# Two graph layers on one core: z_hi and z_lo side by side in one aggregation matmul, degree summed by ScalarE

## What is computed

```python
def _L0(x, adj, W):                      # B=8, N=1024, F=256
    deg = jnp.sum(adj, axis=-1, keepdims=True)
    agg = jnp.einsum('bij,bjf->bif', adj, x) / jnp.maximum(deg, 1e-6)
    out = jnp.einsum('bnf,of->bno', jnp.concatenate([x, agg], axis=2), W)
    return relu(out)
def _L1(X, A, kernel, bias):
    Ah = A + eye(N)
    dh = rsqrt(jnp.sum(Ah, axis=-1))
    An = dh[:, :, None] * Ah * dh[:, None, :]
    return relu(jnp.einsum('bnm,bmf,fc->bnc', An, X, kernel) + bias)
x = layernorm(x + _L0(x, adj, L0_gnn_W))
x = layernorm(x + _L1(x, adj, L1_gnn_kernel, L1_gnn_bias))
```

## Time and profile before

| | |
|---|---|
| median of 3 runs | 513.65 us (513.21 to 514.17) |
| profiled execution, its time | 514.48 us |
| its span, first to last instruction | 512.3 us |
| PE busy | 494.2 us, 96%, 3072 matmuls |
| DVE busy | 388.8 us, 76% |
| ACT busy | 244.3 us, 48% |
| DMA | 59.78 MB, 16 engines 32.7% busy |

### The profile page before, as it was taken

The page is one execution under the profiler, slowest core; times in us unless marked ns, Lnnn a source line. Parts: engine busy times, 40 slices in busy tenths (PEclk is TensorE's granted clock), DMA queues, the critical chain, the costliest instruction groups (busy, mean ns, idle before and its releaser), DMA issues.

```text
span 512.3 us, 8698 instructions
## 1 busy us (share of the span) xinstructions
PE 494.2 (96%) x3072; PEld 446.1 (87%) x3072; DVE 388.8 (76%) x1020; ACT 244.3 (48%) x483; POOL 0.7 (0%) x6
## 2 busy tenths in 40 slices
PE   4999999999999999999999999999999999999992
PEld 3899889988899888998889988998889988899872
DVE  4788487984889847987679858798397984898656
ACT  5735436374283542635444553636437364263312
POOL 0000000000000000000000000000000000000000
PEclk9999999999999999999999999999999999999997
DMA  8944401644018240372305531064401614020002
GB/s 280 377 153 166 157 8 41 210 159 164 0 56 278 75 164 0 104 265 67 137 0 174 223 119 58 0 246 164 164 0 41 246 41 164 0 83 1 0 1 82
DMA packets 15978, 59.78 MB, mean 117 GB/s; under 512 B 1760, under 2 KB 1888, under 8 KB 15072
## 3 DMA queue, kind: packets, MB, share of 16 engines
q1 hardware_dynamic: 15968, 59.64, 32.7%
HBM read 51.25 MB, written 8.39 MB: 116 GB/s over the span
## 4 chain that ended last, share of the span: by engine, by line
PE 96%; DVE 2%; DMA 1%; ACT 0%; SPq 0%; issue 0%; ACTq 0%
PE ring_a L586 24%; PE ring_a L590 12%; PE ring_b L602 11%; PE ring_b L603 11%; PE ring_b L604 11%; PE ring_b L562 6%; PE ring_b L564 6%; PE ring_b L563 6%; PE ring_a L562 3%; PE ring_a L563 3%; PE ring_a L564 3%; DMA x<-w 1%; DVE u L405 0%; DVE stats L414 0%; DVE x L409 0%
## 5 line engine op out<-in xcount | busy, mean ns | idle before, releaser
L586 PE MATMUL ring_a<-z_hi,adj_lo 128*128 128x258 f32 x512 | 103.2, 283 | 0.0
L586 PE MATMUL ring_a<-z_hi,adj_hi 128*128 128x258 f32 x512 | 102.5, 282 | 0.0
L590 PE MATMUL ring_a<-z_lo,adj_hi 128*128 128x256 f32 x512 | 101.3, 279 | 0.0
L602 PE MATMUL ring_b<-adj_hi,x1s_hi 128*128 128x512 f32 x256 | 99.9, 390 | 0.0
L603 PE MATMUL ring_b<-adj_lo,x1s_hi 128*128 128x512 f32 x256 | 99.7, 389 | 0.0
L604 PE MATMUL ring_b<-adj_hi,x1s_lo 128*128 128x512 f32 x256 | 99.7, 389 | 0.0
L586 PEld LDWEIGHTS ring_a<-z_hi,adj_lo 128*128 128x128 f32 x512 | 79.2, 189 | 0.0
L590 PEld LDWEIGHTS ring_a<-z_lo,adj_hi 128*128 128x128 f32 x512 | 79.0, 189 | 0.0
L586 PEld LDWEIGHTS ring_a<-z_hi,adj_hi 128*128 128x128 f32 x512 | 78.1, 188 | 0.1
L346 DVE TENSOR_TENSOR adj_lo<-adj_raw,adj_hi 128x1024 fp32r<-128x1024 f32 x64 | 75.0, 1221 | 3.8 <-ACT adj_hi L223 3.2
L223 ACT ACTIVATE adj_hi<-adj_raw 128x1024 fp32r<-128x1024 f32 x64 | 62.7, 1055 | 0.0
(11 more groups left out here) (66 smaller groups left out, 685.4 us busy)
## 6 DMA issues: line engine op xcount, KB each, us to landing
adj_raw<-adjT SPq DMA_DIRECT2D x64, 512.0 KB, 6.1
x_sb<-x SPq DMA_DIRECT2D x16, 512.0 KB, 4.9
out<-x SPq DMA_DIRECT2D x16, 512.0 KB, 2.6
xt_raw<-xT SPq DMA_DIRECT2D x7, 1024.0 KB, 4.8
x<-w SPq DMA_DIRECT2D x2, 256.0 KB, 4.0
xt_raw<-xT SPq DMA_DIRECT2D x2, 256.0 KB, 4.8
xt_raw<-xT SPq DMA_DIRECT2D x1, 512.0 KB, 6.2
x<-k SPq DMA_DIRECT2D x1, 256.0 KB, 8.9
```

The lines of the kernel that those rows point to most:

```text
L586: nc.tensor.matmul(ring_a[:, t % NB + o, 0:F + 2], adj_block(a, h, j, i0 + o * P, P), z_hi[:, j, :], start=(j == 0 and a is a_hi), stop=False)
L590: last = nc.tensor.matmul(ring_a[:, t % NB + o, 0:F], adj_block(a_hi, h, j, i0 + o * P, P), z_lo[:, j, :], start=False, stop=(j == T - 1))
L602: nc.tensor.matmul(ring_b[:, bank, :], lhi, ahi, start=(j == 0), stop=False)
```

## The change

`z_hi` and `z_lo` become the two halves of one tile `z` of 512 columns. An aggregation step is now one matmul of 512 columns for adj_hi (which gives adj_hi*z_hi in columns 0 to 255 and adj_hi*z_lo in 256 to 511) and one of 256 columns for adj_lo, added onto columns 256 to 511. The columns of ones are gone. DVE adds both halves of the result to `p1`, one after the other. The degree is summed on ACT: the adjacency is loaded a second time in natural layout (`adjN`, 512 KB for each tile of 128 rows, two buffers `nat`), by DMAs that ACT itself issues, and an activation copy with an accumulated output writes `deg`. The large matmul operands start at multiples of 128 bytes; `w_hi` and `w_lo` began in the middle of such a line.

```diff
+        w_hi = sb("w_hi", [P, FT, 2 * F], F32R, LINE)
+        w_lo = sb("w_lo", [P, FT, 2 * F], F32R, LINE)
+        z = sb("z", [P, T, 2 * F], F32R, LINE)
+        z_hi, z_lo = z[:, :, 0:F], z[:, :, F:2 * F]
+        nat = sb("adj_nat", [P, 2, N])
...
+            def load_rows(n, t):
+                i = t % 2
+                nc.scalar.dma_start(nat[:, i, :], adjN[n, :, t, :]).then_inc(nat_loaded[i], 16)
+
+            def degree(n, t, last=False):
+                if not last:
+                    act.wait_ge(deg_done, n * T + t)
+                    load_rows(n + (t + 1) // T, (t + 1) % T)
+                act.wait_ge(nat_loaded[t % 2], 16 * (n * (T // 2) + t // 2 + 1))
+                if not (type(n) is int and n == 0):
+                    act.wait_ge(deg_read, (n - 1) * (T // 2) + t // 2 + 1)
+                nc.scalar.activation(nat[:, t % 2, :], nat[:, t % 2, :], ACT.Copy,
+                                     accum_out=deg[:, t, :]).then_inc(deg_done, 1)
...
                 diagonal(b, 1)
+                if more:
+                    degree(b + 1, 4)
+                    degree(b + 1, 5)
                 read_g(b, 0, 0, 0, 2)
+                if more:
+                    degree(b + 1, 6)
                 read_g(b, 1, 0, 1, 3)
...
+                if t == 1:
+                    load_rows(0, 0)
+                if t >= CH:
+                    degree(0, t - CH)
...
-            split_adj(0, 1)
+            for i in range(CH):
+                split_adj(0, 1, chunks=[i])
+                degree(0, CH + i)
...
                     for o in range(2):
                         nc.vector.scalar_tensor_tensor(
                             p1[:, t + o, :], ring_a[:, bank + o, 0:F], rdeg[:, o, :],
+                            p1[:, t + o, :], ALU.mult, ALU.add).then_inc(main_added, 1)
+                    for o in range(2):
+                        dve.wait_ge(main_added, b * T + t + o + 1)
+                        nc.vector.scalar_tensor_tensor(
+                            p1[:, t + o, :], ring_a[:, bank + o, F:2 * F], rdeg[:, o, :],
                             p1[:, t + o, :], ALU.mult, ALU.add).then_inc(agg_read, 1)
...
-                    for a in (a_hi, a_lo):
-                        for o in range(2):
-                            nc.tensor.matmul(ring_a[:, t % NB + o, 0:F + 2],
-                                             adj_block(a, h, j, i0 + o * P, P), z_hi[:, j, :],
-                                             start=(j == 0 and a is a_hi), stop=False)
                     for o in range(2):
-                        last = nc.tensor.matmul(ring_a[:, t % NB + o, 0:F],
-                                                adj_block(a_hi, h, j, i0 + o * P, P), z_lo[:, j, :],
+                        nc.tensor.matmul(ring_a[:, t % NB + o, :],
+                                         adj_block(a_hi, h, j, i0 + o * P, P), z[:, j, :],
+                                         start=(j == 0), stop=False)
+                    for o in range(2):
+                        last = nc.tensor.matmul(ring_a[:, t % NB + o, F:2 * F],
+                                                adj_block(a_lo, h, j, i0 + o * P, P), z_hi[:, j, :],
                                                 start=False, stop=(j == T - 1))
```

More of the change, by code:

```diff
@@ L20, with gnn_two_layers, sb @@
 PL = 6
+LINE = 128
+HALF = LINE // 8
 DEG_EPS = 1e-6
 LN_EPS = 1e-5
-def gnn_two_layers(nc, adjT, x, xT, w, k, bias, out):
+def gnn_two_layers(nc, adjT, adjN, x, xT, w, k, bias, out):
     ctx = ExitStack()
     with ctx:
-        def sb(name, shape, dt=F32):
-            return ctx.enter_context(nc.sbuf_tensor(name, shape, dt))
+        def sb(name, shape, dt=F32, align=32):
+            return ctx.enter_context(nc.sbuf_tensor(name, shape, dt, align_bytes=align))
         def sem(name):
             return ctx.enter_context(nc.semaphore(name))
+        w_hi = sb("w_hi", [P, FT, 2 * F], F32R, LINE)
+        w_lo = sb("w_lo", [P, FT, 2 * F], F32R, LINE)
+        z = sb("z", [P, T, 2 * F], F32R, LINE)
+        z_hi, z_lo = z[:, :, 0:F], z[:, :, F:2 * F]
+        a_hi = sb("adj_hi", [P, H * T * NH], F32R, LINE)
+        a_lo = sb("adj_lo", [P, H * T * NH], F32R, LINE)
         raw = sb("adj_raw", [P, H, T, NH])
-        a_hi = sb("adj_hi", [P, H * T * NH], F32R)
-        a_lo = sb("adj_lo", [P, H * T * NH], F32R)
+        nat = sb("adj_nat", [P, 2, N])
         diag = sb("adj_diag", [P, T, P])
@@ L58, in gnn_two_layers @@
         p1 = sb("p1", [P, T, F])
[L59 to L62, removed]
+        k_pad = sb("k_pad", [P, HALF], F32, LINE)
         k_hi = sb("k_hi", [P, FT, F], F32R)
@@ L67, in gnn_two_layers @@
         ident = sb("ident", [P, 1, P])
-        ones = sb("ones", [P, T, 2])
+        deg = sb("deg", [P, T, 1])
         deg_c = sb("deg_c", [P, 2, 1])
@@ L102, in gnn_two_layers @@
         x1_free = [sem(f"x1_free{h}") for h in range(H)]
-        ident_zero, ident_done, ones_done = sem("ident_zero"), sem("ident_done"), sem("ones_done")
+        ident_zero, ident_done = sem("ident_zero"), sem("ident_done")
+        nat_loaded = [sem(f"nat_loaded{i}") for i in range(2)]
+        deg_done, deg_read = sem("deg_done"), sem("deg_read")
+        main_added = sem("main_added")
         start_hi_done, start_lo_done = sem("start_hi_done"), sem("start_lo_done")
@@ L111, in gnn_two_layers @@
         z_hi_done, z_lo_done = sem("z_hi_done"), sem("z_lo_done")
-        z_ones_done = sem("z_ones_done")
         proj0_done = sem("proj0_done")
@@ L283, in read_g, with batch @@
                 copy(g_part(True, h, f), ring_b[:, bank, :]).then_inc(g_hi_done, 1)
-            def batch(b, more):
+            def batch(b, more, last=False):
                 if more:
@@ L288, in batch @@
                     split_xt(b + 1)
+                    degree(b + 1, 0)
+                    degree(b + 1, 1)
                 root(b, 0, 2 * TH)
                 diagonal(b, 0)
+                if more:
+                    degree(b + 1, 2)
                 norm0(b, 0)
                 if more:
+                    degree(b + 1, 3)
                     read_proj0(b + 1, 0, 0)
@@ L309, in batch @@
                 if more:
+                    degree(b + 1, 7, last)
                     root(b, 2, TH)
@@ L334, in _ @@
                     split_adj(0, 0, chunks=[t])
+                if t == 1:
+                    load_rows(0, 0)
+                if t >= CH:
+                    degree(0, t - CH)
             act.wait_ge(k_loaded, 16)
             copy(k_hi[:], k_raw).then_inc(k_hi_done, 1)
-            split_adj(0, 1)
-            with act.Fori(0, B - 1) as b:
+            for i in range(CH):
+                split_adj(0, 1, chunks=[i])
+                degree(0, CH + i)
+            with act.Fori(0, B - 2) as b:
                 batch(b, True)
+            batch(B - 2, True, True)
             batch(B - 1, False)
@@ L375, in add_layer0 @@
                     bank = t % NB
-                    degree = ring_a[:, bank:bank + 2, F:F + 1]
-                    dve.wait_ge(agg_done, b * T + t + 2)
-                    nc.vector.tensor_scalar(deg_c[:], degree, DEG_EPS, None,
+                    dve.wait_ge(deg_done, b * T + t + 2)
+                    nc.vector.tensor_scalar(deg_c[:], deg[:, t:t + 2, :], DEG_EPS, None,
                                             ALU.max).then_inc(deg_clamped, 1)
-                    nc.vector.tensor_scalar(v[:, q:q + 2].rearrange("p (q o) -> p q o", o=1), degree,
-                                            1.0, None, ALU.add)
+                    nc.vector.tensor_scalar(v[:, q:q + 2].rearrange("p (q o) -> p q o", o=1),
+                                            deg[:, t:t + 2, :], 1.0, None,
+                                            ALU.add).then_inc(deg_read, 1)
                     dve.wait_ge(deg_clamped, pair)
@@ L384, in add_layer0 @@
                     dve.wait_ge(rdeg_done, pair)
+                    dve.wait_ge(agg_done, b * T + t + 2)
                     for o in range(2):
@@ L522, in batch @@
                     last.then_inc(last_out_done, 1)
-            nc.vector.memset(ones[:], 1.0).then_inc(ones_done, 1)
             nc.vector.memset(deg_c[:], 0.0).then_inc(g_read, 4)
@@ L529, in _ @@
             nc.vector.memset(nb[:], 0.0).then_inc(x1_free[1], 16)
-            dve.wait_ge(ones_done, 1)
-            nc.vector.tensor_copy(z_hi[:, :, F:F + 2], ones[:]).then_inc(z_ones_done, 1)
             for f in range(FT):
@@ L676, in _ @@
                 project0(0, t, t % NB)
-            pe.wait_ge(z_ones_done, 1)
             with pe.Fori(0, B - 1) as b:
@@ L691 @@
         "adjT": adj.reshape(B, H, NH, T, P).transpose(0, 1, 4, 3, 2),
+        "adjN": adj.reshape(B, T, P, N).transpose(0, 2, 1, 3),
         "x": x.reshape(B, T, P, F).transpose(0, 2, 1, 3),
@@ L701 @@
     arrays = {name: np.ascontiguousarray(a) for name, a in arrays.items()}
-    nc = bacc.Bacc("TRN2", target_bir_lowering=False, num_devices=1)
```

(1 more changed line is left out.)

## The result

The changed kernel takes 558.07 us (median of 4 runs, 557.47 to 560.46) where the kernel before takes 513.66 (513.21 to 514.17): a ratio of 1.087 [1.085, 1.089], 44.4 us slower. Forecast were 538.0 us and a range of 517 to 547: the sign was right, the size was not.

What follows compares the result with a forecast made beforehand. PE was taken to bound the kernel, with work on ACT or DVE free only up to their cover. The terms -6.3 + 7 x (1.3 + 1.1) + 13 + 1.5 = +25.0 us gave 538 us, range 517 to 547.

Steps and rivals of the forecast that it cites:

- PE gains 6.3 us: PE's matmuls over the whole program: 5.5 us from merged aggregation matmuls plus 0.8 us from W's alignment in `project0`.
- the merge: Aggregation on PE: three narrow matmuls become a wide and a narrow one, saving 0.69 us a batch, 5.5 us in all.
- W's share: Wide matmuls of `project0`: W beginning on a 128-byte line saves 0.8 us over 384 of them, at the least nothing.
- Place A: DVE ahead of `project0` of tile 4: second additions exceed the cover, stalling PE 1.3 us a batch (0.5 to 1.5).
- Place B: ACT ahead of the first `read_g`: degrees wait for row loads, stalling PE 1.1 us a batch at `project1` of tile 4.
- landing time L: Time from issue to landing of a 512 KB row load beside SP's four loads: 5.2 us, between 3.6 and 6.9.
- Place C: The start: degrees between ACT's tiles and chunks delay the first pair, so PE waits 13 us (5.8 to 18).
- The clock: After PE's long wait in the start, work runs at half speed: 1.5 us lost (0 to 3.5).
- Rival 1: Row loads land quickly, so the batch's load stall vanishes and the start costs 6 to 8: 523 us; chance 0.20.
- rival 2: All added work on DVE and ACT is covered and PE alone decides: 507.4 us; chance 0.06.
- rival 3: A merged 512-column matmul costs what two narrow ones do, with the stalls as forecast: 544 us; chance 0.08.
- rival 4: PE's gain and small stalls in batches and start cancel: within 1 us of 513.65; chance 0.03.

Runs made afterwards that it cites:

- e3: The changed kernel without degree copies, row loads and the second additions on DVE, so its output lacks adj_hi*z_lo: 508.49 us.
- e8: The kernel before with w_hi and w_lo at multiples of 128 bytes and nothing else changed: 515.40 us.
- e12: The changed kernel without degree work and second additions, with z 64 bytes behind a 128-byte line and W still on one: 509.10 us.
- e11: The changed kernel without degree work and second additions, with w_hi and w_lo 64 bytes behind a 128-byte line: 510.04 us.
- e2: The changed kernel without degree copies and row loads, the degree a constant; the second additions stay: 517.75 us.
- e1: The changed kernel with its degree copies but the row loads taken out, two tiles' rows loaded once and summed repeatedly: 523.25 us.
- e5: The changed kernel with four row buffers and each row load issued three degrees ahead instead of one, same traffic: 527.14 us.
- e4: The kernel before with the row loads and degree copies added on ACT at the changed kernel's places, their sum unused: 553.13 us.

## Why the prediction was right in sign and wrong in size

- **What bounds the kernel: right.** PE's waits account for the loss (3.9 us a batch, 13.7 in the start), and they came at places read off the three timelines.
- **PE gains 6.3 us: too large by 1.** e3 gives 5.2. The undisturbed aggregation of e3 lasts 22.3 us and not 22.1, since a wide matmul on z starts every 233 ns, not every 227 as in `propagate`; so the merge gains 8 x 0.51 = 4.1 us of the 5.5 booked. W's share is the 0.8 booked: `project0` goes from 229 to 227 ns, 11.0 to 10.9 us a batch. But its reason, the line, does not hold (e8, e12), so this part was luck. e11's 1.6 us are against an arrangement that is slower than the kernel before, with 233 ns.
- **Place A, 1.3 us a batch: right in the sum, too large at its place.** `project0` waits 0.7 us, and not in seven batches but in five or six. By e2 against e3 the additions cost 9.3 us where 7 x 1.3 = 9.1 were forecast, but spread otherwise: nothing in the first interval (60.6 us in both), 1.4 in each later one, of which 0.35 stand in the aggregation, ahead of its third pair. An addition cost what its row said: the second two of a pair of tiles start 0.80 us behind the first two, at 177.87 and 177.07.
- **Place B, 1.1 us a batch: this is the step that failed.** The wait was the one described, but the landing time L was set at 5.2 us, from SP's loads alone; beside SP's burst it was 5.9 and 8.1. And only the last `read_g` was taken to keep PE waiting. With 5.9 and 8.1 us in the prediction's own chain, degree 5 is over at 188.8, degree 6 at 192.7, and `read_g` 1 is subtracted at about 193.9. PE wants it for the *first* `project1` at 191.77 - 0.8 + 1.3 = 192.3: a wait of 1.6 us, which the prediction did not have, since with 5.2 it was covered by 0.9 us. The split then begins 6.2 us late and not 3.6, and the last `read_g` is done at 207.0 where PE comes at 204.9: 2.1 us. Measured are 1.2 and 2.0. So B is 3.2 us a batch. Without the loads (e1) and with the loads issued earlier (e5) both waits go. With the degree work alone (e4) the later one stays and the first does not come, since it needs A's delay of DVE too: the two places are not independent terms of a sum.
- **Place C, 13 us: right.** The gaps less one matmul each are 13.7 us. The clock cost more than the 1.5 taken, some 2.9 by rows, half of the 5.9 us that PE worked at half speed: PE worked 2.8 us at half speed behind the long wait, as forecast, and another 3 us in 30.61 to 34.02 behind a wait of 3.4 us, and two of the later batches had such a stretch too. With the first batch's own waits this makes +19.3 for the first interval, where the prediction's terms give 16.1.
- **The books.** Forecast +25, measured +44.5 by the spans. Six periods of +4.3 on average in place of +1.6 are 16 us of the difference, the first interval 3. Of the 2.7 us a period B makes 2.1; the rest is the smaller gain, what additions and waits cost beside it, and the half-clock stretches.
- **The rivals.** Rival 1 (loads land quickly) is refuted by the landing times, rival 2 (all covered) by e2, rival 3 (no gain from the merge) by e3, rival 4 (gain and stalls cancel) by the result itself. The range was too narrow on the slow side: B's seven waits are one unknown, L, taken seven times. At its upper row of 6.9 the prediction's own B was 2.8 us a batch, 7 x 1.7 = 12 us more, 550 and thus outside the range of 547. I had called the far ends unlikely, as if they were independent.

## What to carry to other kernels

A load that is issued one step ahead of its use costs its landing time at every use, on an engine that may be half idle. Size it by the landing time beside the other queue's burst at that instant, not alone, and look for each consumer behind the waiting engine, not the last only. A range over terms that share an unknown has to be taken with that unknown at its end in all of them. And where PE is busy for nearly the whole span, work moved off PE pays only if the engine that takes it has cover at that place: here 9.3 us of additions stood against 5.2 us of matmul.

## What the runs showed of the hardware

- 512 KB landed in 3.6 us alone on SP's queue and in 3.7 on ACT's, and after 5.9 and 8.1 us beside 2 MB of the other queue; issued earlier, as in e5, it still took 6.0.
- Behind a wait of 0.5 to 1.9 us the successor of the first matmul started 0.11 us late, in all three places of the batch shown.
- A matmul of 512 columns went every 226 to 236 ns, depending on where its operands lie (e3, e11, e12).
